# Scatter-adding the last 12 experts' rows by token in a mixture-of-experts layer, with the six choice sets loaded and added meanwhile

## The reference, cut to what matters

```python
x = _layernorm(x + attn(x))
router_logits = x @ gate_w.T
topk_w, topk_idx = jax.lax.top_k(softmax(router_logits), 6)
topk_w = topk_w / sum(topk_w)
combine = sum(one_hot(topk_idx, 64) * topk_w[..., None], axis=1)      # token x expert
h = silu(einsum('th,eih->tei', x, experts_w1))
y = einsum('tei,ehi->teh', h, experts_w2)
routed_out = einsum('teh,te->th', y, combine)
x = _layernorm(x + routed_out + shared_out)
```

## Time and profile before

| | us |
|---|---|
| median of 3 runs | 265.72 (263.58 to 265.8) |
| the profiled execution, whole | 266.17 |
| its span, first to last instruction | 264.4 |

### The profile page before, as it was taken

How to read it: one execution, slowest core, us unless ns; L and a number is a source line. 1 busy time by engine, 2 the same in 40 slices (tenths; PEclk the granted TensorE clock), 3 DMA queues, 4 the chain that set the end, 5 groups by cost and what they waited for, 6 DMA issues and landing times.

```text
span 264.4 us, 4056 instructions
## 1 busy us (share of the span) xinstructions
PE 206.9 (78%) x1332; PEld 162.5 (61%) x1332; DVE 126.5 (48%) x385; ACT 94.2 (36%) x177; POOL 127.6 (48%) x126
## 2 busy tenths in 40 slices
PE   3999979929939889973999999999999999900000
PEld 2868757827534767852688888888888877600000
DVE  1337959786867755343243333333333213026794
ACT  2244375625453272000223333333333335430024
POOL 3005252796784776760133555555555567750000
PEclk9999999986986999997799999999999999975555
DMA  7999999996733233557848999999999822289804
GB/s 258 320 427 427 428 430 371 408 403 212 316 133 104 103 135 117 186 191 224 319 138 253 359 400 403 385 391 392 379 397 396 313 78 75 75 313 382 334 15 146
DMA packets 30199, 73.61 MB, mean 278 GB/s; under 512 B 4584, under 2 KB 15450, under 8 KB 28512
## 3 DMA queue, kind: packets, MB, share of 16 engines
q1 hardware_dynamic: 24224, 57.71, 58.8%
q0 software_dynamic: 5376, 14.56, 14.8%
q10 hardware_dynamic: 576, 1.05, 1.1%
HBM read 46.70 MB, written 28.70 MB: 285 GB/s over the span
## 4 chain that ended last, share of the span: by engine, by line
PE 53%; DVE 15%; DMA 11%; POOL 7%; issue 7%; ACT 4%; SPq 1%; POOLq 0%; ACTq 0%; DVEq 0%
PE bank L517 10%; PE bank L716 9%; PE bank L730 9%; PE bank L736 5%; PE bank L723 5%; PE bank L701 5%; DMA shared_mem<-part_rows 3%; PE bank L609 3%; POOL slot_rows L321 3%; DMA xg<-slot_rows 3%; DMA part_rows<-shared_mem,rid 3%; POOL part_rows L342 3%; DVE x L866 2%; PE bank L577 2%; PE bank L554 1%
## 5 line engine op out<-in xcount | busy, mean ns | idle before, releaser
L342 POOL DMA_INDIRECT part_rows<-shared_mem,rid x64 | 62.3, 973 | 56.4 <-ACT shared_mem L472 42.1
L321 POOL DMA_INDIRECT slot_rows<-x,slot x48 | 50.6, 1055 | 24.1 <-issue 13.3
L988 DVE COPY shared_mem<-bank 128x512 f32<-128x512 f32 x32 | 22.0, 688 | 70.9 <-PE bank L701 70.8
L465 ACT ACTIVATE shared_mem<-bank 128x384 f32<-128x384 f32 x32 | 15.0, 490 | 82.9 <-PE bank L723 82.9
L517 PE MATMUL bank<-xT,win 128*128 128x256 f32 x160 | 40.6, 413 | 4.4 <-DMA xT<-x_t 4.4
L517 PEld LDWEIGHTS bank<-xT,win 128*128 128x128 f32 x160 | 32.7, 208 | 10.3 <-DMA win<-w_in 4.3
L472 ACT ACTIVATE shared_mem<-bank,wts 128x256 f32<-128x256 f32 x64 | 25.4, 474 | 4.9 <-PE bank L736 4.9
L716 PE MATMUL bank<-shared_mem,w1s 128*128 128x128 f32 x192 | 24.9, 282 | 1.2 <-DVE shared_mem L988 1.2
L716 PEld LDWEIGHTS bank<-shared_mem,w1s 128*128 128x128 f32 x192 | 23.5, 198 | 1.7 <-issue 1.7
L730 PE MATMUL bank<-w2s,shared_mem 128*128 128x256 f32 x96 | 24.2, 392 | 0.0
L609 PE MATMUL bank<-x1T,guw 128*128 128x256 f32 (+3 forms) x72 | 24.1, 486 | 0.0
(11 more groups left out here) (131 smaller groups left out, 270.9 us busy)
## 6 DMA issues: line engine op xcount, KB each, us to landing
slot_rows<-xg SPq DMA_DIRECT2D x1, 10752.0 KB, 35.8
xg<-slot_rows SPq DMA_DIRECT2D x32, 336.0 KB, 6.7
w2s<-w SPq DMA_DIRECT2D x24, 384.0 KB, 9.1
w1s<-w SPq DMA_DIRECT2D x24, 352.0 KB, 7.3
hsh<-w SPq DMA_DIRECT2D x4, 384.0 KB, 6.8
hsh<-w SPq DMA_DIRECT2D x4, 352.0 KB, 5.7
win<-w_in SPq DMA_DIRECT2D x5, 256.0 KB, 6.7
xT<-x_t ACTq DMA_DIRECT2D x4, 256.0 KB, 5.7
```

The costliest lines, as they stand in the source:

```text
L321: nc.gpsimd.indirect_dma_start(rows_dram, bass.IndirectOffsetOnAxis(ap=slot[:, n:n + 1], axis=0), x1[:, t, :], None, bounds_check=E * P - ...
L342: nc.gpsimd.indirect_dma_start(part_dram, bass.IndirectOffsetOnAxis(ap=rid[:, e:e + 1], axis=0), ysb[:, e % U, :], None, bounds_check=T * ...
L988: v.tensor_copy(xgT[:, j % UP, :], bank[j % 2][:, 0:2 * D]).then_inc(xt_copied, 1)
```

## The change

- Experts 0 to 51 write their rows to the six sets as before. Experts 52 to 63 (`LATE = 12`) write theirs into two new sums of [1024, 256], even experts into one and odd ones into the other, by token, with an indirect DMA whose `compute_op` is add. Two such adds to the same sum may not overlap, so from expert 54 on GpSimd waits for the landing of put e-2 before it issues put e.
- `part_dram` (6.29 MB) must now be zero where a late expert would have written, and the two sums (2 x 1.05 MB) must be zero too: three DMAs from `xg`, behind the weights of the first ten pairs in SP's queue. SP waits for them before the first `load_rows`, and GpSimd before the first put.
- All six sets are loaded as soon as puts 44 to 51 have landed (the sixth when the first add is done). The vector engine adds all six whole, so six adds of 128 x 2048 stand in L1018's place, and not five and four quarters.
- When the third add and `routed_done` are there, SP loads the two sums in four groups, two DMAs of 256 KB for each group, and `last_add(g)` has two adds of 128 x 512 before the statistics.
- `look` finds the token number instead for the late experts, with as many instructions as before. Three tiles of the fallback go.

```diff
+LATE = 12
+CW = TB * D
@@ SP, behind the loop that loads the first ten pairs' weights
+            zeros = xg[:].rearrange("p u w -> p (u w)")[:, None, 0:TT * D]
+            sp.dma_start(part_dram.rearrange("(p k n) d -> p k (n d)", p=P, k=K), zeros.broadcast_to([P, K, TT * D])
+                         ).then_inc(sums_zeroed, 16)
+            for i in range(2):
+                sp.dma_start(sum_dram[i].rearrange("(p n) d -> p (n d)", p=P), zeros[:, 0]).then_inc(sums_zeroed, 16)
+            sp.wait_ge(sums_zeroed, 48)
             sp.wait_ge(scattered, 16 * (TT - TB) * K)
@@ SP, tail
+            for e in range(E - LATE - U, E - LATE):
+                sp.wait_ge(put[e % U], 16 * (e // U + 1))
             for k in range(K):
-                if k == 0:
-                    for e in range(E - K - U + 1, E - K + 1):
-                        sp.wait_ge(put[e % U], 16 * (e // U + 1))
-                else:
-                    sp.wait_ge(put[(E - K + k) % U], 16 * ((E - K + k) // U + 1))
                 if k == K - 1:
                     sp.wait_ge(parts_used, 1)
-                for h in range(2 if k == K - 1 else 1):
-                    n = TD // 2 if k == K - 1 else TD
-                    sp.dma_start(parts[k][:, h * n:(h + 1) * n], rows[k][:, h * n:(h + 1) * n]
-                                 ).then_inc(parts_loaded[k + h], 16)
+                sp.dma_start(parts[k], rows[k]).then_inc(parts_loaded[k], 16)
+            sp.wait_ge(parts_used, 3)
+            sp.wait_ge(routed_done, 1)
+            for g in range(TT // TB):
+                for i in range(2):
+                    sp.dma_start(parts[1 + i][:, g * CW:(g + 1) * CW],
+                                 sum_dram[i].rearrange("(p t) d -> p (t d)", p=P)[:, g * CW:(g + 1) * CW]
+                                 ).then_inc(sums_loaded[g], 16)
@@ GpSimd, put_rows
+                if e < E - LATE:
+                    nc.gpsimd.indirect_dma_start(part_dram, where, ysb[:, e % U, :], None,
+                                                 bounds_check=T * K - 1, oob_is_err=False).then_inc(put[e % U], 16)
+                else:
+                    if e >= E - LATE + 2:
+                        pool.wait_ge(put[(e - 2) % U], 16 * ((e - 2) // U + 1))
+                    nc.gpsimd.indirect_dma_start(sum_dram[e % 2], where, ysb[:, e % U, :], None, compute_op=ALU.add,
+                                                 bounds_check=T - 1, oob_is_err=False).then_inc(put[e % U], 16)
+
+            pool.wait_ge(sums_zeroed, 48)
@@ vector engine, look
+                else:
+                    link(v.tensor_reduce(found[:], same[:], AX_X, ALU.add))
+                    link(v.scalar_tensor_tensor(found[:], xg[:, u:u + G, XI + 7], -MISS, found[:], ALU.add, ALU.mult))
@@ vector engine, tail
-            for k in range(K - 1):
+            for k in range(K):
                 dve.wait_ge(parts_loaded[k], 16)
                 v.tensor_tensor(flat, flat, parts[k], ALU.add).then_inc(parts_used, 1)
                 dve.wait_ge(parts_used, k + 1)
 
             def last_add(g):
-                dve.wait_ge(parts_loaded[K - 1 + g // 2], 16)
-                c = slice(g * TB * D, (g + 1) * TB * D)
-                link(v.tensor_tensor(flat[:, c], flat[:, c], parts[K - 1][:, c], ALU.add))
+                dve.wait_ge(sums_loaded[g], 32)
+                c = slice(g * CW, (g + 1) * CW)
+                for i in range(2):
+                    link(v.tensor_tensor(flat[:, c], flat[:, c], parts[1 + i][:, c], ALU.add))
```

More of the change, by code:

```diff
@@ L66, in build @@
     part_dram = nc.dram_tensor("part_rows", [T * K, D], F32).ap()
+    sum_dram = [nc.dram_tensor(f"late_sum{i}", [T, D], F32).ap() for i in range(2)]
     with ExitStack() as ctx:
@@ L203, in build @@
         routed_done = sem("routed_done")
[L204 removed]
+        sums_zeroed = sem("sums_zeroed")
         over_zidx = sem("over_zidx")
@@ L210, in build @@
         over_added = sem("over_added")
-        over_step = sem("over_step")
         sp_turn = sem("sp_turn")
-        parts_loaded = [sem(f"parts_loaded{i}") for i in range(7)]
+        parts_loaded = [sem(f"parts_loaded{i}") for i in range(6)]
+        sums_loaded = [sem(f"sums_loaded{i}") for i in range(4)]
         parts_used = sem("parts_used")
@@ L341, in put_rows @@
                 pool.wait_ge(y_copied, e + 1)
-                nc.gpsimd.indirect_dma_start(part_dram, bass.IndirectOffsetOnAxis(ap=rid[:, e:e + 1], axis=0),
-                                             ysb[:, e % U, :], None, bounds_check=T * K - 1, oob_is_err=False
-                                             ).then_inc(put[e % U], 16)
+                where = bass.IndirectOffsetOnAxis(ap=rid[:, e:e + 1], axis=0)
+                if e < E - LATE:
[7 more added lines that the diff above has]
+            pool.wait_ge(sums_zeroed, 48)
             for e in range(E):
@@ L353, in _ @@
             with pool.If(over > 0):
[L354 to L357, removed]
-                    nc.gpsimd.indirect_dma_start(part_dram, bass.IndirectOffsetOnAxis(ap=over_z[:, n:n + 1], axis=0),
-                                                 ysb[:, 0, :], None, bounds_check=T * K - 1, oob_is_err=False
-                                                 ).then_inc(over_step, 16)
-                pool.wait_ge(over_step, 16 * TT * K)
                 pool.wait_ge(over_added, E * (TT + 1))
@@ L976, in look @@
                                      ALU.is_equal))
-                link(v.tensor_tensor(same[:], same[:], xg[:, u:u + G, XI:XI + 8], ALU.mult))
-                link(v.tensor_reduce(found[:], same[:], AX_X, ALU.add))
+                if g * G < E - LATE:
+                    link(v.tensor_tensor(same[:], same[:], xg[:, u:u + G, XI:XI + 8], ALU.mult))
+                    link(v.tensor_reduce(found[:], same[:], AX_X, ALU.add))
+                else:
+                    link(v.tensor_reduce(found[:], same[:], AX_X, ALU.add))
+                    link(v.scalar_tensor_tensor(found[:], xg[:, u:u + G, XI + 7], -MISS, found[:], ALU.add, ALU.mult))
                 for j in range(G):
@@ L997, in _ @@
                 v.tensor_scalar(over_w[:], fits[:], -1.0, 1.0, ALU.mult, ALU.add).then_inc(over_zidx, 1)
[L998 removed]
+                dve.wait_ge(over_zidx, 1)
+                v.tensor_tensor(over_w[:], over_w[:], x1[:, :, XC:XC + E], ALU.mult).then_inc(over_zidx, 1)
                 dve.wait_ge(over_zidx, 2)
[L1000 to L1005 removed]
                 with dve.Fori(0, E // 2) as n:
```

11 lines of the change are left out of this document (1 added, 10 removed).

## The result

The changed kernel takes 285.39 us (281.51 to 285.83), the kernel before 265.76 on the same chip: a ratio of 1.068, with a 95% interval from 1.053 to 1.082. It is slower, as forecast, but by 19.6 us and not by 9.4, outside the range of 266 to 283. The profiled execution has a span of 282.9 us and took 284.96 in all.

A forecast was written before the change was run, and what follows sets the result against it. The prediction took the transfer of six 1 MB sets behind the last puts as the bound. Put 63's landing at 254.4 plus 19.4 gave 273.8 against 264.4; 265.72 + 9.4 = 275.1, said 275, range 266 to 283.

The forecast's parts named there:

- the zeroing: Zeroing DMAs beside the attention's compute: 8.39 MB from 66 to about 99 us, hidden, cost 0.
- the chain of adding puts: Puts 52 to 63 on GpSimd: puts e and e + 2 in series, put 63 landing at 254.4 us.
- a dear add, or a deeper queue: Rival: DMA add costs 2.3 us, 6 us more in all, or five queued sets add 3.8 us; chance 0.20.
- the landings beside the set loads: Late puts while sets load: put 52 lands unhindered in 3.1 us, loaded landings take 6.5, the add inside.
- The unhindered round: Late puts after the loads: 0.7 us release to row start, then 3.1 to landing, 0.8 of it the add.
- The pairing: End of the put chain: put 63 starts 1.3 us behind put 62, at 251.3, and lands at 254.4.
- The stretched rows: GpSimd's put rows beside the vector engine's whole adds: 0 to 2.1 us lost a put, mean 0.4 a round.
- The tail: Behind put 63's landing: 1.0 us hand-over, 3.3 for the first group's loads, 15.1 for the last part; 19.4 us.
- Overtaking: Rival: puts slip between the set loads' packets and land in 2.3 us, end 261.4, 3.0 us faster; chance 0.08.

The follow-up runs named there:

- e1: Kernel before, plus only the three zeroing DMAs (8.39 MB) and the two waits for them: 279.38 us against 280.46, ratio 0.995.
- e12: Changed kernel with at most two set loads queued: ratio 1.049 to the kernel before.
- e2: Changed kernel with plain writes in place of the adds for experts 52 to 63, waits kept: 284.58 us, ratio 1.015 to the kernel before.
- e0: The changed kernel itself run again, on a slower chip: 294.44 us against 279.83 for the kernel before, ratio 1.054.
- e8: Changed kernel with a tensor for each late expert, plain writes and no waits for put e-2: 270.48 us against 265.08 before, ratio 1.018.
- e6: Changed kernel with each set load issued only when the one before has landed: ratio 1.042 to the kernel before.
- e11: Changed kernel with set loads one by one and whole adds cut into four: 294.6 us against 283.35 for the kernel before, ratio 1.040.
- e5: Changed kernel with each set load cut into four loads of 512 columns (2 KB descriptors): ratio 1.059 to the kernel before.
- e10: Changed kernel with own tensors, plain writes, no waits and whole adds cut into four: 280.53 us against 283.35 for the kernel before, ratio 0.990.
- e15: Same version as e10, run on one chip with the uncut-add version (280.49 us): 276.31 us, ratio 0.988 to the kernel before.

## Why the prediction was wrong in size

**Right in kind.** The change does what it says; the zeroing is hidden (e1); the first set load starts at 221.08, forecast near 222; the new end is the chain of adding puts; the vector engine idles before the first group, 22.8 us where I had 12. The rival "a dear add, or a deeper queue", at 0.20, comes near in time if both its halves are added up (281 and 3.8 more), but neither half happened as written, so that would be luck. The unhindered add cost 1.4 us and not 2.3; of the landings behind the loads only put 57's took 5 us, and that with a row stretched by the last whole add. The deeper queue did not count: two sets held a put almost as long as five (e12).

**The step that failed: the landings beside the set loads.** The working let put 52 land unhindered, in 3.1 us, although its own first set load starts 1 us behind that put, and it took 6.5 us with "the add inside" for the puts after it. Put 53, which starts wholly beside the loads, had no price at all. Measured: 8.07 us for put 52, 9.8 for put 53, 8.95 and 9.2 for puts 54 and 55. For plain puts 6.5 was right (6.4 to 6.75 in e2), and a plain put 52 does slip through in 2.3. The add had no price of its own beside the loads, though I had given it 0.8 on a free queue; put for put, e2 against e0, it is 2.5 to 3.5 us there. The odd puts decided the end. Along them the chain was 41.8 us, against my 33.3:

| | forecast, us | measured, us |
|---|---|---|
| start behind put 52's | 1.3 | 1.9 |
| first landing (put 52 forecast, put 53 measured) | 3.1 | 9.8 |
| next round | 7.6 | 10.0 |
| next two rounds | 13.7 | 10.9 |
| last two rounds | 7.6 | 9.2 |

Of the 8.5 us, 6.7 are the first landing alone and 2.4 the second. The loads ended at 241.8 and not at 244, which gave 2.8 back.

**The unhindered round, 3.8 us.** Measured about 4.6 (253.44 to 258.04): a landing of 3.73 and not 3.1, and 0.83 from release to row and not 0.7. The add costs 1.4 us, 0.6 of it in GpSimd's own row (1.55 against 0.97), which I had left at 0.97.

**The pairing.** I let put 63 follow put 62 by 1.3 us. In the trace the odd puts ran 2.7 to 3.8 us behind the even ones from put 55 on, since put 53 was caught behind the loads that put 52 escaped in part.

**The stretched rows, 0.4 us a round.** In the changed kernel one row counts, 3.01 us at 242.51 beside the last whole add. My mean was near enough there, because GpSimd mostly waits. But for the idea it was far too small: 10 us in the free chain (e8). The Trainium skill, "SBUF — State Buffer", section "Who interferes with whom", says that the ports which the vector engine and GpSimd share are an exclusive lock, and that a vector instruction with two SBUF inputs contends with a GpSimd instruction that reads SBUF; the stretched rows of e8, each ending 0.85 us behind its add, agree.

**The tail, 19.4 us.** Measured 21.1: 1.25 (261.77 to 263.02) for `routed_done`, 3.9 to the first group and not 3.3, and 16.0 and not 15.1 (266.90 to 282.9), 0.7 of it a wait for the second group's load that I had called hidden. The start was 1.1 us early. Together: -1.1 + 8.5 (41.8 against 33.3) + 1.7 = 9.1, the 282.9 measured less the 273.8 forecast.

**Why the gain was so small.** The working held it, and I didn't say it: the tail behind put 63 shrinks only from 22.9 us to 19.4 by my own numbers, so 3.5 us was the most that the whole change could give, against a chain that had to grow not at all. Measured, it was 1.8.

**Overtaking** (0.08) fell: while several sets were queued, puts 53 and 54 landed in no version in under 6.2 us, though 2.35 us is what a plain put takes unhindered. Only with one set queued at a time did some adding puts land in 3.7 to 3.9 us (e6, e11), about their unhindered time. The Trainium skill, "DMA: Bandwidth & Descriptors", section "Queues, rings and completion order", states that a DMA engine drains a whole packet from one queue, 9 to 17 descriptors as a rule, before it turns to the next. I had read this as a small wait. An estimate from that figure: at 383 GB/s over 16 engines a descriptor of 8 KB takes 0.34 us, so one turn of the other queue is 3.1 to 5.8 us, and a plain put lost 4.0 to 4.4 (6.4 to 6.75 less 2.35). So with loads of such descriptors that rule doesn't speak for overtaking. For descriptors of 2 KB it would be a quarter, 0.8 to 1.5 us, and there the trace doesn't agree: adding puts in e5 lost 3.6 to 4.3 us (7.35 to 8.0 less 3.73).

## What to carry to other kernels

Before moving work out of a tail, subtract the two tails: what follows the last dependent step before and after is all the gain there is (here 1.8 us), and any growth of that step's chain comes off it. A scatter that adds, in which each call must wait for an earlier one's landing, turns landing time from a delay into a rate: count the rounds, and price a landing beside whatever bulk transfer the same change puts there, not beside idle DMA engines. Look also at what stands first in the chain: the first put was priced unhindered, and that alone was 6.7 of the 8.5 us by which the chain was missed. Where the tail is bound by a transfer, fewer bytes (1.5% here, with bf16 rows) did what an earlier start could not.

## What the runs showed of the hardware

- An indirect DMA of 128 rows of 1 KB that adds has a row of 1.55 us on GpSimd and lands in 3.73 us; a plain one 0.97 and 2.35 (empty slots among the 128 are not written). Beside saturated DMA engines with 8 KB descriptors the same puts took 9.1 to 10.0 us with the add (e0) and 6.4 to 6.75 without (e2). The adding ones moved in packets of 1 KB, the plain ones in packets of 4 KB.
- Two 1 MB loads in the other queue delay an adding put almost as much as five do (8.1 to 9.5 us against 8.3 to 10.0); one delays it less, to 3.9 to 6.75. For puts 53 to 55, four loads a set with descriptors of 2 KB gave 7.35 to 8.0 us, and four with 8 KB 10.0 to 12.0, at a lower rate of the loads themselves (238 against 321 GB/s).
- GpSimd's row for a plain indirect DMA that begins while a float32 add with both inputs in SBUF runs on the vector engine ends 0.85 us behind that add (six of six in e8): at most 2.89 us there beside adds of 2.29, at most 1.50 beside adds of 0.69 (e10, e15). A row that begins before the add is not stretched (put 58 in e8, 0.97 us; puts 55 and 56 in the changed kernel, 1.54 and 1.55 us).
- The same program took 265 us on some chips and 280 to 283 on others; at a full DMA share in the expert stage they carried 392 to 393 and 358 to 369 GB/s. Only ratios on one chip could be compared.
